# A low-rank end in scaled fp16 with DMA transpositions, and another order of the prologue, in a one-layer kernel on one core

## What is computed

```python
# h: S4D kernel; 128 heads, 64 modes, 32 channels x, length 1024
V = exp(dtA[:, :, None] * ell);  K = 2.0 * einsum('chn,hnl->chl', Cc, V).real
h = K
h = h + layernorm(h) @ W_attn.T + b_attn
x = layernorm(h)
gates = softmax(x @ Wr.T)                    # 4 experts
proj_r = einsum('bsi,eri->bser', x, A)       # rank 8 each
lora = einsum('bse,bseo->bso', gates * 2.0, einsum('bser,eor->bseo', proj_r, Bm))
h = h + x @ W_ffn.T + b_ffn + lora
```

## Time and profile before

| | us |
|---|---|
| median of 3 runs | 815.11 (813.63 to 816.08) |
| the profiled execution | 816.2, span of its instructions 814.4 |
| PE busy | 778.5 (96% of the span), mean granted clock 0.987, from 40 to 60 us 0.74 |
| DVE, ACT busy | 626.2 (77%), 527.2 (65%) |
| DMA moved | 72.28 MB, mean 89 GB/s |

### The profile page before, as it was taken

One profiled execution on the slowest core, in us unless ns is written; L12 is line 12 of the kernel. 1 busy time (PEld: TensorE's weight loads), 2 busy tenths in 40 slices (PEclk: granted clock), 3 DMA queues, 4 the chain that ended last, 5 costly groups with the idle time before them and its releaser, 6 DMA issues.

```text
span 814.4 us, 14994 instructions
## 1 busy us (share of the span) xinstructions
PE 778.5 (96%) x5390; PEld 390.9 (48%) x5390; DVE 626.2 (77%) x1250; ACT 527.2 (65%) x884; POOL 5.5 (1%) x22
## 2 busy tenths in 40 slices
PE   2788799999999999999999999999999999999998
PEld 2644344444444444445444444544445444444443
DVE  7789897787778877877788778777887787778522
ACT  6777786766677675757676676767767575765210
POOL 2000000000000000000000000000000000000000
PEclk9879999999999999999999999999999999999999
DMA  7838643345333242434233333433324243423223
GB/s 276 300 72 153 120 87 77 81 69 97 77 66 82 55 93 60 89 77 91 59 75 73 77 78 70 97 77 64 82 55 96 57 91 77 90 52 74 56 52 77
DMA packets 185708, 72.28 MB, mean 89 GB/s; under 512 B 174096, under 2 KB 179088, under 8 KB 185560
## 3 DMA queue, kind: packets, MB, share of 16 engines
q1 hardware_dynamic: 185592, 71.90, 40.5%
q10 hardware_dynamic: 96, 0.13, 0.0%
HBM read 14.06 MB, written 16.78 MB: 38 GB/s over the span
## 4 chain that ended last, share of the span: by engine, by line
PE 89%; DVE 5%; issue 3%; SPq 2%; DMA 1%; ACT 1%; POOLq 0%; POOL 0%; DVEq 0%; ACTq 0%
PE ps_g L490 39%; PE ps_g L550 39%; PE ps_a L481 6%; PE ps_g L561 2%; PE ps_g L682 1%; PE ps_p L538 1%; DMA bias_bc<-in_L_attn_bias 1%; SPq L347 1%; DVE stage L1219 1%; SPq L402 1%; PE ps_p L540 1%; DVE wa_lo L1211 0%; PE ps_p L555 0%; DVE h_tok L1081 0%; DVE h_tok L1120 0%
## 5 line engine op out<-in xcount | busy, mean ns | idle before, releaser
L490 PE MATMUL ps_g<-wa_hi,x 128*128 128x512 f16 x1024 | 271.0, 380 | 2.3 <-DMA x<-x_tok 1.7
L550 PE MATMUL ps_g<-wf_hi,x 128*128 128x512 f16 x992 | 265.1, 380 | 0.4 <-DVE h_tok L1120 0.4
L490 PEld LDWEIGHTS ps_g<-wa_hi,x 128*128 128x128 f16 x1024 | 97.9, 98 | 123.1 <-issue 7.7
L490 PE MATMUL ps_g<-wa_lo,x 128*128 128x512 f16 x512 | 154.1, 380 | 0.0
L550 PE MATMUL ps_g<-wf_lo,x 128*128 128x512 f16 x496 | 149.2, 380 | 0.0
L550 PEld LDWEIGHTS ps_g<-wf_hi,x 128*128 128x128 f16 x992 | 95.0, 98 | 107.2 <-issue 2.1
L1182 DVE SCALAR_TENSOR_TENSOR result<-ps_g,unscale,h_tok 128x1024 f32<-128x1024 f32 x31 | 39.8, 1283 | 84.2 <-PE ps_g L561 84.2
L753 ACT ACTIVATE junk<-ps_a,stat 128x1024 bf16<-128x1024 f32 x32 | 35.6, 1114 | 76.9 <-DVE stat L1084 76.9
L490 PEld LDWEIGHTS ps_g<-wa_lo,x 128*128 128x128 f16 x512 | 50.2, 98 | 60.4 <-issue 0.5
L550 PEld LDWEIGHTS ps_g<-wf_lo,x 128*128 128x128 f16 x496 | 48.5, 98 | 58.4 <-issue 0.3
L759 ACT ACTIVATE junk<-h_tok,stat 128x1024 bf16<-128x1024 f32 x32 | 36.7, 1148 | 59.2 <-DVE stat L1124 59.2
(11 more groups left out here) (209 smaller groups left out, 920.8 us busy)
## 6 DMA issues: line engine op xcount, KB each, us to landing
out<-result SPq DMA_DIRECT2D x124, 128.0 KB, 2.2
stage<-in_L_ffn_W SPq DMA_DIRECT2D x8, 512.0 KB, 12.8
x_raw<-in_x SPq DMA_DIRECT2D x38, 64.0 KB
wf_hi<-in_x SPq DMA_DIRECT2D x1, 2048.0 KB, 10.7
h_tok<-in_L_attn_weight SPq DMA_DIRECT2D x2, 512.0 KB, 3.8
x<-in_L_attn_weight SPq DMA_DIRECT2D x2, 512.0 KB, 6.6
result<-in_L_attn_weight SPq DMA_DIRECT2D x2, 512.0 KB, 7.9
x<-x_tok SPq DMA_TRANSPOSE x64, 3.2
```

The source lines that it names most:

```text
L490: mm = pe.matmul(ps[:, o, :], x1_part(part, ps is ps_g2)[:, k, :], ws[:, k, o * HALF:(o + 1) * HALF], start=k == 0 and part == 0 and ws is ...
L550: pe.matmul(ps_g2[:, o, :], xs[:, k, :], ws[:, k, o * HALF:(o + 1) * HALF], start=k == 0 and xs is x2_hi and ws is wf_hi, stop=False)
```

## The change

The low-rank end is done in plain fp16 with power-of-two scales, and its two transpositions are made by DMA. `lora_split`, `lora_t` are 128x128 in fp16 and `lb` is 128x8x128 in fp16. To keep the numbers in fp16's range, the projections are scaled by `lora_down` as they are read from PSUM, B by `lora_up`, and the bias by a column of 2^15; the scales come from new maxima (`bound_lora_b`, `join_bias_top`, `lora_scales` on DVE, one wider reduction on POOL). `turn_lora` and `turn_lora_b` move from PE to SP; `copy_lora` on DVE and ACT's two copies of `lb` are gone. Around this the hand-written order changes on every queue.

```diff
@@ SP
+            def turn_lora(t, i):
+                at_least(sp, s_g2, 2 * t + i)
+                sp.wait_ge(s_soft, 6 * (2 * t + i) + 6)
+                sp.dma_start_transpose(lora_t[:, :].unsqueeze(1), lora_split[:, :]).then_inc(s_lora_t, 16)
+            def turn_lora_b():
+                sp.wait_ge(s_lbn, 3)
+                sp.dma_start_transpose(lb[:, :, :], lbn_rows.bitcast(F16)).then_inc(s_lbt, 16)
-            load_weight(0, 3)
+            load_weight(0, 2)
+            sp.dma_start(bias_bc[:, :], attn_b.unsqueeze(0).broadcast_to((P, L))).then_inc(s_bias, 16)
             sp.dma_start(x_all, x.rearrange("c (b h) n r -> (c b) (h n r)", b=4)).then_inc(s_x_all, 16)
             load_x(0)
-            load_weight(3, 6)
-            sp.dma_start(bias_bc[:, :], attn_b.unsqueeze(0).broadcast_to((P, L))).then_inc(s_bias, 16)
-            load_weight(6, 16)
+            load_weight(2, 16)
...
+            turn_weights(9, 10)
             turn_x1(0, 1)
-            turn_weights(9, 13)
+            turn_weights(10, 13)
+            turn_lora_b()
             turn_x2(0, 0)
             turn_weights(13, 16)
+            turn_lora(0, 0)
@@ PE
             def ffn_end(t, i):
-                pe.wait_ge(s_lora_sb, 2 * t + i + 1)
+                pe.wait_ge(s_lora_t, 16 * (2 * t + i + 1))
                 for o in range(2):
-                    mm = pe.matmul(ps_g2[:, o, :], lora_t[:, :], lb[:, o * HALF:(o + 1) * HALF],
-                                   start=False, stop=True)
+                    mm = pe.matmul(ps_g2[:, o, :], lora_t[0:KL, :], lora_rows(o), start=False, stop=True)
...
             project(0, 0)
-            pe.wait_ge(s_lb_sb, 2)
+            s4(1, 0)
             pe.wait_ge(s_wf_0, 32)
             pe.wait_ge(s_wf[0], 96)
             pe.wait_ge(s_h2, 2)
             ffn_part(0, 0, range(0, 3), (0,))
-            s4(1, 0)
@@ ACT
             rstd_guess(0, 0, stat_1, s_ssq1, s_log1, s_y1, m_eps)
             phases(0, 1)
-            attn_hi(2)
+            attn_hi(2, 3)
             high_1(0, 0)
-            attn_hi(3)
             decays(0, 1)
...
             high_1(1, 0)
+            high_2(0, 1)
             decays(1, 1)
             sines(1, 1)
-            high_2(0, 1)
@@ DVE
-            attn_lo(2)
             round_turns(0, 1)
-            attn_lo(3)
+            attn_lo(2, 3)
             low_1(0, 0)
+            bound_lora_b()
             dve.wait_ge(s_lo1, 1)
             weight_norms(1, ps_p[:, 0:P])
-            split_scales(1)
+            join_bias_top()
...
             low_1(0, 1)
+            lora_scales()
             ffn_lo(10)
             split_lora_b()
...
             keep_h2(0, 0)
             round_turns(1, 0)
+            normalise_2(0, 0)
             ffn_lo(14)
-            normalise_2(0, 0)
             low_2(0, 0)
...
             make_m(1, 0)
+            make_u(1, 0)
             dve.wait_ge(s_wf_0, 32)
             keep_h2(0, 1, ps_g2)
-            make_u(1, 0)
```

More of the change, by code:

```diff
@@ L127, in program @@
         lora = sb("lora", [P, ER])
-        lora_split = sb("lora_split", [P, KL], F32R)
-        lora_t = sb("lora_t", [KL, P], F32R)
+        lora_split = sb("lora_split", [P, P], F16)
+        lora_t = sb("lora_t", [P, P], F16)
         params = sb("params", [P, 1280])
@@ L440, in _ @@
                         turn_x1(*after(t, i))
+                    turn_lora(*before(t, i))
                     turn_x2(t, i)
             t = TILES - 1
+            turn_lora(t, 1)
             store(t, 0)
@@ L569, in turn_lora_a @@
                 mm.then_inc(s_wg_t, 1)
[L571 to L578, removed]
             pe.wait_ge(s_const, 3)
@@ L644, in _ @@
             ffn_part(0, 0, range(0, 3), (1,))
-            turn_lora(0, 0)
             ffn_part(0, 0, range(3, KB), (1,))
+            pe.wait_ge(s_lbt, 16)
+            ffn_end(0, 0)
             turn_x(2)
-            ffn_end(0, 0)
             def step(t, i):
@@ L654, in step @@
                 project(*b)
-                ffn_part(*b, range(0, 6))
-                turn_lora(*b)
-                ffn_part(*b, range(6, KB))
+                ffn_part(*b, range(KB))
                 ffn_end(*b)
@@ L669, in _ @@
             project(t, 0)
-            ffn_part(t, 0, range(0, 6))
-            turn_lora(t, 0)
-            ffn_part(t, 0, range(6, KB))
+            ffn_part(t, 0, range(KB))
             ffn_end(t, 0)
@@ L875, in _ @@
                            scale=scale[:, 1:2]).then_inc(s_wg_hi, 1)
-            for o in range(2):
-                act.wait_ge(s_lbt, o + 1)
-                act.activation(lb[:, o * HALF:(o + 1) * HALF], ps_g1[0:KL, o, :], ACT.Copy).then_inc(s_lb_sb, 1)
-            decays(1, 0)
+            act.wait_ge(s_wlo, low_done(8))
+            high_2(0, 0)
+            ffn_hi(15)
             sines(1, 0)
@@ L905, in step @@
                 rstd_guess(t, i, stat_2, s_ssq2, s_log2, s_y2)
+                gate_exp(*before(t, i))
                 if waves:
                     high_u(t + 1, i)
-                gate_exp(*before(t, i))
                 high_2(t, i)
@@ L1229, in finish_last, with bound_lora_b @@
                     .then_inc(s_result_last, 1)
+            def bound_lora_b():
+                dve.wait_ge(s_lb, 16 * (KB + 1))
+                dve.wait_ge(s_bias_dve, 1)
+                rows, squares = params[:, 0:KB * ER], params[:, 780:780 + KB * (ER + 1)]
+                dve.memset(lbn[:, :, KL:P], 0.0)
+                dve.scalar_tensor_tensor(out=squares[:, KB:], in0=rows, scalar=1.0, in1=rows, op0=ALU.mult,
+                                         op1=ALU.mult, accum_out=top[:, 3:4]).then_inc(s_lb_top, 1)
+                dve.tensor_scalar(lbb, lbb, bias_stat[:, 1:2], None, ALU.subtract).then_inc(s_lb_top, 1)
+                dve.wait_ge(s_lb_top, 2)
+                dve.scalar_tensor_tensor(out=squares[:, 0:KB], in0=lbb, scalar=1.0, in1=lbb,
+                                         op0=ALU.mult, op1=ALU.mult, accum_out=bias_square).then_inc(s_lb_top, 1)
```

142 lines of the change are left out of this document (80 added, 62 removed).

## The result

The new kernel took 809.16 us (median of 5, 808.2 to 810.2) beside 816.08 us for the kernel before (median of 5, 813.63 to 818.15): a ratio of 0.9917, 95% interval 0.9899 to 0.9936, so 6.9 us less. A second time, beside other executions of the kernel before (815.4), it took 808.97: 0.9923, 0.9904 to 0.9942. Forecast were 808.1 and a range of 804.0 to 812.2. The profiled execution took 809.99 around a span of 808.1, 6.3 us less than the 814.4 of before.

The account below looks back on a forecast made before the run. PE, busy 96% of the span, was taken to bound the kernel, with waits in prologue and tail. Steps -5.1, prologue -2.5 and tail +0.6 sum to -7.0 us: 808.1 from a median of 815.1, range 804.0 to 812.2.

Parts of the forecast that it names:

- Steady steps: 30 steps on PE, each 0.17 us shorter (0.14 to 0.23) from a period of 23.28: 5.1 us gained (4.2 to 6.9).
- the pair's gain: Low-rank matmul pair in each step: fp16 instead of fp32r gains 0.13 us, or 0.04 where projections follow the pair.
- The transfer in the steps: DMA of lora_split in each step lands between 424.95 and 426.1, wanted at 427.53: margin 1.4 to 2.6 us, costed at nothing.
- Prologue: Start of the kernel up to the S4 product (1,1): 2.5 us gained, bounds 4.5 gained and 0.5 lost.
- (a): Prologue up to 40 us: bias load moves ahead of x, weight block 2 behind it; costed at nothing.
- (b): Prologue, DVE at 41.77: rounding now stands ahead of attn_lo(2), so attn_lo(3) ends at 42.2 instead of 43.05, 0.9 us earlier.
- The second attention product starts no sooner: Prologue: turn_x1(0,1), now behind block 9's low part on SP, takes back 0.9 us on that transfer.
- (c): Prologue, DVE from low_1(0,1) to make_u(1,0): 19.3 us instead of 21.1; S4 product (1,0) starts at 82.5, not 87.05.
- (d): Prologue, from there to make_u(1,1): 16.2 us instead of 14.7; S4 product (1,1) starts at 98.7, 3.0 us earlier.
- The clock: Prologue gap before 98.7: if PE falls to 1.2 GHz, some 3 us at half speed cost 1.5; a third was charged.
- Tail: Last step: x2's low half and the last lora_split transfer may make PE wait; 0.6 us lost (0.1 gained to 1.3 lost).
- The three sums: Whole kernel: steady steps -5.1, prologue up to the first steady step -2.5 and tail +0.6, added to -7.0 us.

Follow-up runs that it names:

- the fp32r experiment: New kernel with ffn_end's pair in fp32r on constant zeros in all half-tiles but the last: period 23.17 us, 29 steps 671.5 us against 670.8.

## Why the prediction was right, point by point

**The total: right, to 0.1 us by luck.** Forecast 7.0 us less, measured 6.9. But the 7.0 were taken from a median of 815.1, and the 6.9 from one of 816.08; the kernel before alone spreads over 4.5 us in that series. In the two profiled spans it is 6.3: the steps gave 1.2 less than forecast, the tail took 0.4 less, and the prologue agrees in the execution read first, where several errors cancel.

**Steady steps: mechanism right, size high.** Forecast 5.1 us for 30 steps, measured 3.9 over 29 of them: 0.13 a step, not 0.17. The term that was mis-sized is the pair's gain, bounded by 0.04 and 0.13 and taken in between (0.07). The trace and the fp32r experiment give 0.02 to 0.03. Of the 0.56 us reckoned for the fp32r pair, 0.53 are there with an fp16 pair too (423.25 to 423.78). Fp16 pairs followed by others of their kind stand 0.43 apart, so 0.10 of the 0.53 belong to the start of the S4 product. The right comparison was already in the earlier trace rows: the same follower behind both kinds of pair.

**The transfer in the steps: right.** `lora_split` was complete where `gate_end` was said to end, landing took 2.3 us (forecast 2.0 to 3.1), the margin is 2.1 us (forecast 1.4 to 2.6), and PE never waits. That a step pays what exceeds the margin is borne out by the experiment that moved the issue behind x2 (1.42 us in the step read). The Trainium skill's rule ("VectorE: DVE Perf Modes", section "Rules for kernel authors") would have kept the transposition on TensorE; here that costs PE 0.11 us in every step, and the DMA costs it none. Its 1309 ns for the DMA path ("The three transpose paths") lies below the 2.3 us from issue to landing in this trace, and the measurement decides.

**Prologue: sum right by luck, steps wrong.** Forecast -2.5, in the profiled spans -2.6 up to the S4 product (2,0). In the new kernel's second execution it is -4.2, and with the gaps of both kernels filled -1.7; all three lie within the stated bounds.

- (a) "nothing" failed. The loads are worth about 1.7 us in the new order by the medians, 1.9 at the first S4 product: ACT's copy of q stands behind the bias. I had noted that ACT gets its bias earlier, and not asked what is queued behind it.
- (b) the right 0.9 us at block 3's low part, for the wrong reason: with the loads moved, the rounding can stand in either place, and with the old loads its new place wins nothing (43.51). What followed was more than 0.9: `low_1(0,1)` came 3.0 us earlier (59.92 against 62.88), as the half clock behind the gap ended sooner in this execution (1.9 us earlier in the second, 61.01). "The second attention product starts no sooner" was wrong with it: 66.08, not 67.67.
- (c) right in its length: 19.6 us from the end of `low_1(0,1)` (61.15) to the end of `make_u(1,0)` (80.75), forecast 19.3. The S4 product (1,0) starts at 80.80 and not at 82.5 only for (b).
- (d) 16.8 us to the end of `make_u(1,1)`, forecast 16.2: the S4 product (1,0), for which DVE waits, took 1.2 us longer at half clock. In the second execution, at full clock, it is 15.8 from one product's start to the other's.
- The clock: I charged 0.5 us for it, a third of 1.5, and no row stands behind the 3 us of half clock in that. From the S4 product (1,1) to (2,0) it is 25.2 us in the new kernel and was 23.7: 1.5 lost there, so 4.1 gained became 2.6. In the second execution nothing was lost there (23.6). What I missed is the other side: the kernel before loses 4.2 us of its median to its gaps, which I had taken as fixed. With the gaps filled in both, the new prologue is worth 1.7 us.

**Tail: right.** Forecast 0.6 lost, measured 0.2, within its bounds. x2 was late by 0.51, the last `lora_t` by nothing, and 0.3 us came back behind that.

**Additivity: the unstated step.** The three sums were made as if each part of the change stood alone. Alone, the low-rank end gains 3.7 us and loses them in the prologue, and the order gains nothing clear of the noise. That the sum held rests on their being made together.

## What to carry to other kernels

Before costing a change in a prologue full of waits, look how the kernel's executions spread with the mean granted clock: a gap's price is its length and what runs at half speed behind it, and this can be taken away by unread matmuls without any reordering. To price an instruction on a saturated engine, compare start to start with the same follower behind both kinds, not durations. And test parts that seem to add separately: the added work on DVE, which made `low_2(0,0)` 1.2 us late in the old order, went with 3.6 us at the start of the steps there, part of them by the clock, and was hidden in the new order. Last, profile the same kernel twice before reading a few microseconds from a prologue.

## What the runs showed of the hardware

The same program, on the same inputs, ran 813.3 us at a mean granted clock of 0.995 and 819.5 at 0.983. In the profiled executions of near-identical code, gaps of 2.6 us at 40 us were followed by a first group of transpositions at full clock (1.09 us) and half clock behind it, or by half clock at once (1.97 us in the second execution of the new kernel). The length of a gap alone doesn't decide: ahead of the S4 product (1,1) the new kernel waited 2.47 us in its second execution and the product took 1.93 us, and with the rounding moved back it waited 2.48 us and the product took 3.52. Filling the gaps put the mean clock at 0.999 to 1.000 in the new kernel. A DMA transposition of one 128x128 fp16 tile occupied SP's queue for 1.12 us and landed after 2.3; one eight times as large took 1.23 to 1.34 and 3.2, so that most of both is a cost that the size doesn't change here.
